# One more weight unit per attention step, and residual loads from another queue, in an attention and ternary-FFN kernel

## The chip, the cores and the metric

The kernel runs on the 8 cores of one Trainium2 chip. Each core computes one of the 8 sequences of the batch; there is no traffic between the cores. The metric is the time on the device of the slowest core, in microseconds.

## The reference

```python
x = L0_attn_x                                  # (8, 2048, 1024), one sequence a core
x = _layernorm(x + attn(x, w_qkv, w_proj, b_proj))     # 16 heads of 64, softmax over 2048 keys
x = _layernorm(x + ffn(x, w_gate, w_up, w_down))
return x

# grouped_linear: 8 groups of 128 channels, used for qkv (128 -> 384) and proj (128 -> 128)
def _weight_quant(w):                          # ternary weights, one scale for a matrix
    scale = 1.0 / clip(mean(abs(w)), 1e-5)
    return clip(round(w * scale), -1, 1) / scale
def _act_quant(x):                             # 8-bit activations, one scale for a token
    scale = 127.0 / clip(max(abs(x), axis=-1), 1e-5)
    return clip(round(x * scale), -128, 127) / scale
def _bitlinear(x, w):
    return einsum('bsi,oi->bso', _act_quant(x), _weight_quant(w))
# ffn: bitlinear(silu(bitlinear(x, w_gate)) * bitlinear(x, w_up), w_down), 1024 -> 4096 -> 1024
```

## The kernel before

The program is written by hand as five queues of instructions. A helper, `Emitter`, records every instruction under its engine, and `replay` (line 84, which is why nearly every row of the profile says L84) issues them. Engines run their own instructions strictly in the order in which they were recorded; what orders them against each other is written out as waits on semaphore counts. A wait marked `future=True` is for a count that is reached by an instruction recorded later. A DMA is issued by one of three engines: "sync" (SyncE, SPq in the profile), "scalar" (ScalarE, ACTq) or "gpsimd" (GpSimd, POOLq). The issue stands in that engine's order too.

A core's 2048 tokens are T = 16 tiles of 128. The stages:

1. Loads, the bias, bf16 copies of `x`, the transposed copy, and the sums of absolute weights (`emit_wmean`) for the scale of each weight matrix. Then q, k and v.
2. Attention, in QC = 4 blocks of 512 queries (`qc`), each in 8 pairs of heads (`p`), each over 16 key tiles (`kc`): TensorE makes scores, ScalarE the exponential of 128x1024 scores, TensorE the product with v. At the end of a `p` ScalarE copies the result out and sends the row sums by a small DMA (`A10`, sums of all heads of the `qc`). After the eight pairs VectorE takes the reciprocal of `A10` and runs the projection's 64 instructions on 128x128 blocks with TensorE, and then the layer norm of four tiles (`emit_ln_quad`), which writes `xp_s` (the residual for the FFN) and `xq_s` (quantised tokens) to HBM through GpSimd's queue. SyncE then loads `xqT`, the transposed `xq_s`. The first scores of the next `qc` come on TensorE after this `qc`'s projection.
3. Weight quantisation, recorded into the attention so that VectorE and SyncE do it between. The weights are 96 units of 128x1024: `_wq_units` in the order wd, wg, wu, 32 of each. `drain_wq(k)` records k of them. A unit is a load by SyncE into one of two halves of `A5` (`emit_wq_load`, recorded two units ahead; it waits until the unit two before is done), three VectorE instructions of 128x1024 (in the profile `TENSOR_SCALAR A<-A,wsc` is the first of the three, so it marks a unit), and a store by SyncE. `drain_wt(k)` records k of 32 transposed loads of quantised wd (`wtstage<-wdq_s`, SyncE), whose blocks GpSimd stores to `wdqT_s`; it returns at once while fewer than 32 units have been recorded. The calls stand at the end of each `p`:

```python
            if qc == wsum_qc and p == 2:     # wsum_qc = 1
                emit_wsum_once()
            if _wsum_done[0] and p < 7:
                drain_wq(6)
            if qc >= 1 and p < 7:
                drain_wt(4)
```

So calls are made at p = 2 to 6 of qc 1 and at p = 0 to 6 of qc 2 and qc 3 while units are left.

4. Gate and up matmuls (`emit_gu`), twice, for 8 tiles of tokens each (s = 0 and 1): `h = silu(gate) * up`, quantised and stored to `hq_s` by ScalarE's queue.
5. Down matmuls and the last layer norm (`emit_down`), in four token groups of four tiles (`gbase` 0 to 3). TensorE runs over 32 weight tiles (`wdt_sb`, loaded by SyncE four ahead, with transposed loads of `hqT` between) into all eight PSUM banks. Then VectorE adds the residual `xre_f` for tile after tile. `xre_f` holds two tiles, so it is loaded in two pairs from `xp_s`: the first pair when the group before has stored its output, the second when VectorE has used the first (`c_r2` counts tiles). Then follow sums, Squares on ScalarE (which overwrite `xre_f`), and the output `y` through `xre_f`. TensorE's next group waits for VectorE's four tiles.

Of the kernel before, what the change touches and what calls it, by code (L numbers as in the profile page):

```python
# [20 lines left out]
class Emitter:  # L21
# [17 lines left out]
    def c(self, name):  # L39
        self.sem(name)  # L40
        return self.cnt[name]
# [11 lines left out]
    def wait(self, eng, semname, val, future=False):  # L53
        if val <= 0:
            return
        self.sem(semname)
        if future:
            self.future_waits.append((eng, semname, val))
        else:
            assert val <= self.cnt[semname], \  # L60
                f"wait {eng} {semname}>={val} but only {self.cnt[semname]} emitted"
        lw = self.last_wait[eng].get(semname, -1)
        if val <= lw:
            return
        self.last_wait[eng][semname] = val
        self.ops[eng].append(("wait_ge", (self.sems[semname], val), {}, None))
# [6 lines left out]
    def dma(self, eng, out, in_, semname, **kw):  # L73
        return self.emit(eng, "dma_start", out, in_, inc=(semname, 16), **kw)
# [20 lines left out]
def build(T=16, NST=2, debug=False, phase=3, attn_lvl=4):  # L95
# [41 lines left out]
    def alloc(name, shape, dtype, at=None):  # L137
        nbytes = int(np.prod(shape[1:])) * mybir.dt.size(dtype)
        nbytes = (nbytes + 31) // 32 * 32
        if at is None:  # L140
            at = off[0]
            off[0] = at + nbytes
        assert at + nbytes <= 229344, f"SBUF overflow: {name}"
        return nc.alloc_sbuf_tensor_at(name, list(shape), dtype, offset=at), at
# [41 lines left out]
    xre_f, _ = alloc("xre_f", [128, 2048], F32, at=A13o)  # L186
# [13 lines left out]
    def bank(i, lo=0, hi=512):  # L200
        return ps[:, 512 * i + lo: 512 * i + hi]
# [4 lines left out]
    E = Emitter(nc, ctx)  # L206
    em, wait, dma, c = E.emit, E.wait, E.dma, E.c
# [175 lines left out]
    def emit_wq_load(gidx):  # L383
        mi, tii, to = _wq_units[gidx]
        par = gidx % 2
        stg = A5[:, par * 1024:(par + 1) * 1024]
        if gidx >= 2:
            wait("sync", "c_wq3", 3 * (gidx - 1), future=True)
        else:
            wait("sync", "c_wma", 96, future=True)  # L390
        dma("sync", stg, tii, f"s_wqp{par}")

    def drain_wq(k):
        for _ in range(k):
            gidx = _wq_emitted[0]
            if gidx >= len(_wq_units):
                return
            _wq_emitted[0] = gidx + 1
            mi, tii, to = _wq_units[gidx]
            par = gidx % 2  # L400
            stg = A5[:, par * 1024:(par + 1) * 1024]
            obuf = A6[:, par * 1024:(par + 1) * 1024]
            if gidx == 0:
                emit_wq_load(0)
                emit_wq_load(1)
            if gidx + 2 < len(_wq_units):
                emit_wq_load(gidx + 2)
            wait("vector", f"s_wqp{par}", 16 * (gidx // 2 + 1))
            wait("vector", "c_wsc", 1)
            wait("vector", "c_wq3", c("c_wq3"))  # L410
            em("vector", "tensor_scalar", stg, stg, wsc[:, mi:mi + 1], 1.0,
               ALU.mult, ALU.min, inc=("c_wq3", 1))
            wait("vector", "c_wq3", c("c_wq3"))
            em("vector", "tensor_scalar", stg, stg, -1.0, MAGIC, ALU.max, ALU.add,
               inc=("c_wq3", 1))
            wait("vector", "c_wq3", c("c_wq3"))
            if gidx >= 2:
                wait("vector", f"s_wqs{par}", 16 * (gidx // 2))
            em("vector", "tensor_scalar", obuf, stg, MAGIC, None, ALU.subtract,
               inc=("c_wq3", 1))  # L420
            wait("sync", "c_wq3", c("c_wq3"), future=True)
            dma("sync", to, obuf, f"s_wqs{par}")
# [224 lines left out]
    for qc in range(QC):  # L647
        for p in range(8):
# [75 lines left out]
            if qc == wsum_qc and p == 2:  # L724
                emit_wsum_once()
            if _wsum_done[0] and p < 7:
                drain_wq(6)
            if qc >= 1 and p < 7:
                drain_wt(4)
            if qc == 0 and p == 2 and attn_lvl in (3, 4):  # L730
# [260 lines left out]
    def emit_down(s):  # L991
        for tg in range(NTG):
            gbase = s * NTG + tg
            row0 = (s * ST + tg * 4) * 128
            wait("gpsimd", "s_xps0", 16 * (T // 2))
            wait("gpsimd", "s_xps1", 16 * (T // 2))
            if gbase >= 1:
                wait("gpsimd", "c_r2", gbase * 4, future=True)
                wait("gpsimd", "c_s", c("c_s"), future=True)
                wait("gpsimd", "s_out0", 16 * 2 * gbase)  # L1000
                wait("gpsimd", "s_out1", 16 * 2 * gbase)
            for t4 in range(2):
                E.dma("gpsimd", xre_f[:, t4 * 1024:(t4 + 1) * 1024],
                      xp_s[row0 + t4 * 128: row0 + (t4 + 1) * 128, :], "s_xre")
            for jc in range(32):
                k = gbase * 2 + jc // 16
# [37 lines left out]
            for t4 in range(4):  # L1044
                tt = s * ST + tg * 4 + t4
                if t4 == 2:
                    wait("gpsimd", "c_r2", gbase * 4 + 2, future=True)
                    for t4b in range(2, 4):
                        E.dma("gpsimd", xre_f[:, (t4b - 2) * 1024:(t4b - 1) * 1024],
                              xp_s[row0 + t4b * 128: row0 + (t4b + 1) * 128, :],  # L1050
                              "s_xre")
                wait("vector", "c_dn", c("c_dn"))
                wait("vector", "c_v", c("c_v"))
                wait("vector", "c_s", c("c_s"))
                wait("vector", "s_xre", 16 * (gbase * 4 + (t4 // 2) * 2 + 2),
                     future=True)
                xrh = xre_f[:, (t4 % 2) * 1024:(t4 % 2 + 1) * 1024]
                em("vector", "scalar_tensor_tensor", B[t4][:, 0:512],
                   bank(t4 * 2), scd[:, tt:tt + 1], xrh[:, 0:512],
                   ALU.mult, ALU.add, inc=("c_dne", 1))  # L1060
                em("vector", "scalar_tensor_tensor", B[t4][:, 512:1024],
                   bank(t4 * 2 + 1), scd[:, tt:tt + 1], xrh[:, 512:1024],
                   ALU.mult, ALU.add, inc=("c_r2", 1))
# [67 lines left out]
    else:  # L1131
        emit_hqt_half(0)
        emit_hqt_half(1)
    emit_down(0)
    if NST > 1:
        emit_down(1)
# [39 lines left out]
```

How the kernel before makes its waits and increments, by code:

```python
                def body(eng):  # L79
                    for meth, args, kw, inc in self.ops[name]:
                        if meth == "wait_ge":
                            eng.wait_ge(*args)
                        else:
                            ins = getattr(eng, meth)(*args, **kw)
                            if inc is not None:
                                ins.then_inc(*inc)
```

## Time and profile before

| | |
|---|---|
| median of 3 runs (lowest, highest) | 2122.22 us (2120.99, 2122.87) |
| the profiled execution | 2119.69 us |
| its span, core 5, the slowest | 2116.7 us |
| spans of the eight cores | 2109.0 to 2116.7 us |
| granted TensorE clock, mean of a core | 0.844 to 0.846 |
| busy share of the span: TensorE, ScalarE, VectorE, GpSimd | 64%, 45%, 44%, 3% |

All rows below are of core 5. A time is in us from the span's start. In the timeline a row is: start, us taken (of all its instructions, if several are merged as x8), engine, line, operation, output<-inputs with shapes, count, and in brackets how long the engine had been idle before it and who ended that. In the table of waits a row is: who waited for whom, us in total, times, the longest. In a row of windows: the stretch, its length, busy us (and instructions) of PE (TensorE), PEld (its weight loads), DVE (VectorE), ACT (ScalarE) and POOL (GpSimd), the granted TensorE clock as a share of full speed, the busy share of the 16 DMA engines, and GB/s. `A` stands for any of the buffers A0 to A15.

### The profile page before, as it was taken

The numbers are of one execution on the slowest core, as the hardware profiler recorded it, in microseconds if no ns is written. First come the engines' busy times: TensorE is split into PE (matmuls) and PEld (weight loads), VectorE is DVE, ScalarE is ACT, GpSimd is POOL, SyncE is SP. The second block draws the span as 40 slices with busy tenths as digits, with TensorE's granted clock in tenths as the row PEclk, the third lists the DMA queues.
The fourth block names the chain that finished last, engine by engine and source line by source line (L and its number), as shares of the span: only waits on it lengthen the run. The fifth ranks groups of instructions, "written<-read, shape, count | busy, mean of one in ns | idle before, by whom it ended". The sixth has DMA issues, their size and how long they took to land.

```text
span 2116.4 us, 20559 instructions; the slowest of 8 cores (2109.0 to 2116.7 us)
## 1 busy us (share of the span) xinstructions
PE 1342.5 (63%) x5439; PEld 463.1 (22%) x5502; DVE 924.7 (44%) x1742; ACT 948.8 (45%) x1079; POOL 53.1 (3%) x100
## 2 busy tenths in 40 slices
PE   0057767576647773067663799945999728676581
PEld 0001111111111110011111344412444313232230
DVE  1138850554567434484518444444444441303123
ACT  2167888488838884058870112264121461001011
POOL 0000000000000000000000000000000000000000
PEclk9999888688868887578875899977999868898896
DMA  6779960135742777836803633334344416676662
GB/s 184 226 232 327 313 208 1 40 100 151 196 138 79 198 226 211 236 98 174 237 23 96 136 76 76 74 107 120 75 95 95 115 82 166 169 205 185 188 201 77
DMA packets 371458, 314.02 MB, mean 148 GB/s; under 512 B 296593, under 2 KB 298641, under 8 KB 369298
## 3 DMA queue, kind: packets, MB, share of 16 engines
q1 hardware_dynamic: 339712, 234.97, 42.4%
q10 hardware_dynamic: 20882, 39.99, 5.5%
q0 software_dynamic: 10752, 37.75, 4.8%
q8 instruction: 47, 0.77, 0.2%
q14 instruction: 65, 0.53, 0.1%
HBM read 161.49 MB, written 83.89 MB: 116 GB/s over the span
## 4 chain that ended last, share of the span: by engine, by line
PE 43%; ACT 15%; DMA 13%; DVE 12%; SPq 7%; issue 7%; ACTq 2%; DVEq 1%; POOL 0%; POOLq 0%
PE ps L84 43%; ACT A L84 14%; DVE A L84 8%; SPq L84 7%; DMA A<-wg 3%; DMA wdt_sb<-wdqT_s 2%; DVE ln_sb L84 2%; DMA wtstage<-wdq_s 2%; ACTq L84 2%; DMA xre_f<-xp_s 1%; DVE h L84 1%; DMA A<-x 1%; DMA wdqT_s<-wtstage 1%; DMA A<-wu 1%; DMA A<-wqkv 1%
## 5 line engine op out<-in xcount | busy, mean ns | idle before, releaser
L84 ACT ACTIVATE A<-ps,cst_sb 128x1024 bf16<-128x1024 f32 (+1 forms) x544 | 553.1, 1103 | 247.2 <-DVE A L84 157.1
L84 PE MATMUL ps<-A,A 64*128 64x512 bf16 (+1 forms) x2048 | 532.3, 434 | 204.3 <-ACT A L84 180.3
L84 PE MATMUL ps<-wg_sl,xqT 128*128 128x512 bf16 x1003 | 264.0, 407 | 114.6 <-DVE h L84 99.6
L84 PE MATMUL ps<-wdt_sb,hqT 128*128 128x512 bf16 x1003 | 238.3, 393 | 107.2 <-DMA wdt_sb<-wdqT_s 47.7
L84 PEld LDWEIGHTS ps<-A,A 64*128 64x128 bf16 (+1 forms) x2048 | 125.7, 106 | 609.0 <-issue 605.7
L84 ACT ACTIVATE A<-ps,scg 128x512 f32<-128x512 f32 x128 | 87.9, 687 | 331.5 <-PE ps L84 309.5
L84 DVE SCALAR_TENSOR_TENSOR h<-ps,scu,A 128x512 bf16<-128x512 f32 x128 | 96.1, 751 | 216.6 <-ACT A L84 212.4
L84 DVE TENSOR_SCALAR A<-A,wsc 128x1024 f32<-128x1024 f32 x96 | 72.3, 753 | 205.4 <-DMA A<-wg 98.0
L84 PEld LDWEIGHTS ps<-wg_sl,xqT 128*128 128x128 bf16 x1024 | 104.0, 103 | 251.7 <-issue 145.6
L84 DVE TENSOR_SCALAR A<-A 128x1024 f32<-128x1024 f32 (+1 forms) x208 | 144.4, 694 | 32.5 <-DVE A L84 18.2
L84 PEld LDWEIGHTS ps<-wdt_sb,hqT 128*128 128x128 bf16 x1024 | 100.2, 100 | 245.3 <-issue 141.4
L84 ACT ACTIVATE xre_f<-A,ln_sb 128x1024 f32<-128x1024 f32 x16 | 18.4, 1147 | 275.3 <-DVE ln_sb L84 275.3
L84 PE MATMUL ps<-wproj_sb,A 64*128 64x128 bf16 x256 | 36.5, 274 | 155.5 <-DVE A L84 155.5
L84 DVE TENSOR_REDUCE wt<-A 128x1 f32<-128x1024 f32 x96 | 117.1, 1220 | 40.0 <-DMA A<-wg 21.0
L84 ACT ACTIVATE A<-h,cst_sb,ln_sb 128x512 f32<-128x512 bf16 x128 | 104.0, 813 | 56.7 <-DVE scd L84 45.9
L84 PE MATMUL ps<-wu_sl,xqT 128*128 128x512 bf16 x501 | 124.3, 389 | 7.6 <-DMA wu_sl<-wuq_s 7.0
L84 DVE SCALAR_TENSOR_TENSOR A<-ps,scd,xre_f 128x512 f32<-128x512 f32 x32 | 21.8, 745 | 244.6 <-PE ps L84 217.4
L84 PE MATMUL ps<-A,wqkv_sb 128*128 128x512 bf16 x63 | 36.7, 586 | 122.4 <-ACT A L84 76.4
L84 ACT CAST A<-ps 64x512 bf16<-64x512 f32 (+2 forms) x144 | 76.1, 536 | 41.0 <-PE ps L84 37.5
L84 DVE TENSOR_REDUCE A<-h 128x1 f32<-128x512 bf16 x128 | 87.8, 686 | 13.6 <-DVE h L84 0.5
L84 DVE SCALAR_TENSOR_TENSOR A<-ps,A,A 128x128 f32<-128x128 f32 x256 | 78.7, 346 | 16.9 <-PE ps L84 3.1
L84 DVE TENSOR_SCALAR h<-A 128x512 bf16<-128x512 f32 x128 | 54.7, 427 | 65.0 <-ACT A L84 64.9
(67 smaller groups left out, 710.2 us busy)
## 6 DMA issues: line engine op xcount, KB each, us to landing
A<-wg SPq DMA_DIRECT2D x64, 512.0 KB, 5.6
A<-wu SPq DMA_DIRECT2D x64, 512.0 KB, 5.4
A<-wd SPq DMA_DIRECT2D x64, 512.0 KB, 6.4
wdt_sb<-wdqT_s SPq DMA_DIRECT2D x128, 256.0 KB, 3.2
hq_s<-h ACTq DMA_DIRECT2D x16, 1024.0 KB, 3.9
A<-x SPq DMA_DIRECT2D x16, 512.0 KB, 6.9
xt_s<-A POOLq DMA_DIRECT2D x16, 512.0 KB, 3.8
A<-xt_s ACTq DMA_DIRECT2D x16, 512.0 KB, 3.3
```

The source lines that it names most:

```text
L84: ins = getattr(eng, meth)(*args, **kw)
```

## The change

Two things change. The number of weight units recorded at the end of each `p` goes from 6 to 7. In `emit_down` the loads of `xre_f`, with the waits ahead of them, move from GpSimd's queue to ScalarE's. There they stand in ScalarE's order: the first pair after the last work of the stage before (for group 0 after the last `hq_s` store, for the others after the `y` stores of the group before), the second pair ahead of the group's Squares. The wait for `c_s`, ScalarE's own count, is kept.

```diff
@@ -724,7 +724,7 @@
             if _wsum_done[0] and p < 7:
-                drain_wq(6)
+                drain_wq(7)
@@ -992,15 +992,15 @@
-            wait("gpsimd", "s_xps0", 16 * (T // 2))
-            wait("gpsimd", "s_xps1", 16 * (T // 2))
+            wait("scalar", "s_xps0", 16 * (T // 2))
+            wait("scalar", "s_xps1", 16 * (T // 2))
             if gbase >= 1:
-                wait("gpsimd", "c_r2", gbase * 4, future=True)
-                wait("gpsimd", "c_s", c("c_s"), future=True)
-                wait("gpsimd", "s_out0", 16 * 2 * gbase)
-                wait("gpsimd", "s_out1", 16 * 2 * gbase)
+                wait("scalar", "c_r2", gbase * 4, future=True)
+                wait("scalar", "c_s", c("c_s"))
+                wait("scalar", "s_out0", 16 * 2 * gbase)
+                wait("scalar", "s_out1", 16 * 2 * gbase)
             for t4 in range(2):
-                E.dma("gpsimd", xre_f[:, t4 * 1024:(t4 + 1) * 1024],
+                E.dma("scalar", xre_f[:, t4 * 1024:(t4 + 1) * 1024],
                       xp_s[row0 + t4 * 128: row0 + (t4 + 1) * 128, :], "s_xre")
@@ -1044,9 +1044,9 @@
                 if t4 == 2:
-                    wait("gpsimd", "c_r2", gbase * 4 + 2, future=True)
+                    wait("scalar", "c_r2", gbase * 4 + 2, future=True)
                     for t4b in range(2, 4):
-                        E.dma("gpsimd", xre_f[:, (t4b - 2) * 1024:(t4b - 1) * 1024],
+                        E.dma("scalar", xre_f[:, (t4b - 2) * 1024:(t4b - 1) * 1024],
                               xp_s[row0 + t4b * 128: row0 + (t4b + 1) * 128, :],
                               "s_xre")
```

## Rows read from the trace of the kernel before

**Rows 1.** The windows of core 5: qc 2, the boundary, qc 3.
```profile
632.00:818.00 186.00, 131.02 (x507) 31.02 (x506) 92.02 (x140) 157.75 (x160) 13.38 (x24) 0.86 0.64 179
818.00:915.00 97.00, 10.37 (x70) 4.42 (x70) 53.31 (x112) 0.05 (x1) 5.93 (x11) 0.50 0.80 213
915.00:1101.00 186.00, 131.55 (x508) 31.07 (x506) 86.46 (x132) 158.02 (x160) 7.23 (x12) 0.84 0.45 133
```

**Rows 2.** ScalarE's timeline, where attention of qc 2 and qc 3 begins.
```profile
631.78 2.12 ACT L84 ACTIVATE A<-ps,cst_sb 128x1024 bf16<-128x1024 f32 x2 [30.22 <-DVE A L84]
...
914.95 2.12 ACT L84 ACTIVATE A<-ps,cst_sb 128x1024 bf16<-128x1024 f32 x2 [97.29 <-DVE A L84]
```

**Rows 3.** Timeline of VectorE (DVE), from qc 2's last unit to its projection.
```profile
887.65 0.75 DVE L84 TENSOR_SCALAR A<-A,wsc 128x1024 f32<-128x1024 f32 x1 [0.78 <-DMA A<-wu]
...
889.99 0.54 DVE L84 RECIPROCAL A<-A 128x64 f32<-128x64 f32 x1
...
891.35 23.09 DVE L84 SCALAR_TENSOR_TENSOR A<-ps,A,A 128x128 f32<-128x128 f32 x64 [0.82 <-PE ps L84]
```

**Rows 4.** Timeline of VectorE: first and last unit of qc 1, then its projection.
```profile
485.98 0.75 DVE L84 TENSOR_SCALAR A<-A,wsc 128x1024 f32<-128x1024 f32 x1 [1.55 <-ACT wsc L84]
...
599.55 0.75 DVE L84 TENSOR_SCALAR A<-A,wsc 128x1024 f32<-128x1024 f32 x1 [2.18 <-DMA A<-wd]
...
606.80 0.55 DVE L84 RECIPROCAL A<-A 128x64 f32<-128x64 f32 x1 [4.83 <-DMA A<-A]
...
608.17 23.10 DVE L84 SCALAR_TENSOR_TENSOR A<-ps,A,A 128x128 f32<-128x128 f32 x64 [0.82 <-PE ps L84]
```

**Rows 5.** Timeline of VectorE: two units of qc 3, and its reciprocal.
```profile
1016.53 0.75 DVE L84 TENSOR_SCALAR A<-A,wsc 128x1024 f32<-128x1024 f32 x1 [0.97 <-DMA A<-wu]
...
1058.12 0.75 DVE L84 TENSOR_SCALAR A<-A,wsc 128x1024 f32<-128x1024 f32 x1 [0.91 <-DMA A<-wu]
...
1103.57 0.55 DVE L84 RECIPROCAL A<-A 128x64 f32<-128x64 f32 x1 [43.02 <-DMA A<-A]
```

**Rows 6.** Timeline of SyncE's queue (SPq) in qc 2 and after it.
```profile
718.83 0.51 SPq L84 DMA_DIRECT2D A<-wg  x1
...
738.65 11.11 SPq L84 DMA_TRANSPOSE wtstage<-wdq_s  x4
...
891.04 13.18 SPq L84 DMA_TRANSPOSE wtstage<-wdq_s  x4
```

**Rows 7.** Timeline of VectorE: second and last unit of one group.
```profile
727.31 0.75 DVE L84 TENSOR_SCALAR A<-A,wsc 128x1024 f32<-128x1024 f32 x1
...
742.15 0.75 DVE L84 TENSOR_SCALAR A<-A,wsc 128x1024 f32<-128x1024 f32 x1 [0.78 <-DMA A<-wg]
```

**Rows 8.** Timeline at the last `xre_f` reload, and the table of waits.
```profile
2078.02 1.07 POOL L84 DMA_DIRECT2D xre_f<-xp_s  x2 [31.15 <-DVE A L84]
...
2083.00 2.73 DVE L84 SCALAR_TENSOR_TENSOR A<-ps,scd,xre_f 128x512 f32<-128x512 f32 x4 [5.52 <-DMA xre_f<-xp_s]
...
DVE A L84 <- DMA xre_f<-xp_s: 29.5, 4, 9.0
```

**Rows 9.** DMA issues (count, KB each, us to landing); `xt_s` issues, min/median/max ns.
```profile
hq_s<-h ACTq DMA_DIRECT2D x16, 1024.0 KB, 3.9
...
A<-xt_s ACTq DMA_DIRECT2D x16, 512.0 KB, 3.2
...
xp_s<-A POOLq DMA_DIRECT2D x16, 512.0 KB, 3.0
...
L84 ACTq DMA_DIRECT2D A<-xt_s x16: 321/326/685, 269.1 to 1116.7; - x16
```

**Rows 10.** Timeline: an instruction of VectorE, the Square that waits for it.
```profile
2090.54 0.17 DVE L84 TENSOR_SCALAR ln_sb<-ln_sb 128x4 f32<-128x4 f32 x1
...
2090.86 1.15 ACT L84 ACTIVATE xre_f<-A,ln_sb 128x1024 f32<-128x1024 f32 x1 [48.66 <-DVE ln_sb L84]
```

**Rows 11.** The window of the first pass of gate and up.
```profile
1175.00:1463.00 288.00, 240.73 (x1024) 103.95 (x1022) 133.28 (x287) 95.04 (x127) 0.00 (x0) 0.91 0.42 91
```

## The prediction

> **What bounds the kernel now.** I read the page first, then the granted clocks, the windows, the chain of waits, and short stretches of the timeline. By the page no engine is full (TensorE, the busiest, has 64% of the span), so a mean says nothing and the stages have to be looked at one by one.
>
> The windows [rows 1] do that. The attention of qc 2 and of qc 3 take 186 us each, with ScalarE busy 158 us of it: the exponentials set the pace there. Between them lie 97 us in which TensorE is busy for 10.37. ScalarE's own idle time shows how odd that boundary is [rows 2]: ScalarE stood 30.22 us before qc 2, but 97.29 us before qc 3, both times for VectorE, though the projection between is the same 64 instructions in 23.1 us [rows 3, 4].
>
> The reason is the weight quantisation. VectorE runs its instructions in order, and the units of `drain_wq` that the program puts into the attention of a qc stand ahead of that qc's reciprocal and projection. In qc 2 there are 7 calls of 6, 42 units. The last starts at 887.65, and the reciprocal follows its third instruction without a gap, at 889.99 [rows 3]. Attention had been over since about 817.7 (914.95 less 97.29). So in qc 2 the quantisation is the path, by 72 us.
>
> In qc 1 the 30 units end just in time [rows 4]: the first starts at 485.98, the last at 599.55, and it is done 2.4 us later, at 602. The reciprocal then waits 4.83 us for the row sums that ScalarE had just sent, and starts at 606.80. The slack there is those 4.83 us and no more. In qc 3 the last unit starts at 1058.12, and the reciprocal comes at 1103.57, after 43.02 us of idling [rows 5].
>
> **Part 1: `drain_wq(7)` for `drain_wq(6)`.** The work is the same 96 units; only where they stand changes. Before: 5 x 6 = 30 in qc 1, 7 x 6 = 42 in qc 2, 24 in qc 3. After: 35, 49 and 12. That is 5 more in the qc that has 4.83 us of slack, 7 more in the qc that has none, and 12 fewer in the one that had 43 us to spare.
>
> *qc 1.* The rate is 29 intervals in 113.57 us, 3.92 us a unit [rows 4]. Units of wu, in qc 3, run quicker: 12 intervals from 1016.53 to 1058.12, 3.47 us [rows 5]. Of the five, units 30 and 31 are of wd and 32 to 34 of wg, so I take 3.8. Five units are 19.0 us, less the slack of 4.83: **+14.2 us**. The bounds are 5 x 3.47 - 4.83 = 12.5 and 5 x 3.92 - 4.83 = 14.8.
>
> *qc 2.* Here SyncE's queue alternates between the loads and stores of six units and four transposes of `drain_wt(4)` [rows 6]: one group begins at 718.83, its transposes come at 738.65 and hold the queue 11.11 us, and the next group begins at 749.85, 31 us after the first. While the transposes hold the queue no unit is loaded, and VectorE has a hole of over 10 us. One could think the seventh unit free in that hole. It is not: with two staging halves a load is issued only when the unit two before it is done, and the transposes stand in the queue behind the last load and store of the group. A seventh unit pushes the transposes back by one interval, and the hole comes after it, as long as before. The interval inside this group is (742.15 - 727.31) / 4 = 3.71 us [rows 7]; without transposes it is 3.47 [rows 5]. I take 3.6, between the two. Seven groups have one unit more each: **+25.2 us**, with the bounds 7 x 3.47 = 24.3 and 7 x 3.92 = 27.4.
>
> *The transposes.* `drain_wt` does nothing until 32 units are emitted. That is now so at p = 6 of qc 1, so 4 of the 32 transposes move there; 28 stay in qc 2, as before, and the 4 of qc 3 are gone. The moved four stand behind unit 34's store in SyncE's queue and run beside the projection of qc 1. Behind them in that queue is the load of `xqT`, which waits for the end of the layer norm anyway, over 25 us of VectorE's work later. The projection is not slowed by such company: four transposes, from 891.04 on, ran beside that of qc 2, whose 64 instructions took 23.09 us, and those of qc 1 took 23.10 without them [rows 3, 4, 6]. GpSimd stores three of the moved blocks before its next work, the `xp_s` stores of that layer norm. I cost all this at nothing, and keep 3 us as an upper bound.
>
> *qc 3.* The 186 us of attention cover 12 units as they covered 24: nothing.
>
> **Part 2: the loads of `xre_f` go from GpSimd's queue to ScalarE's.** There are 16 loads in 8 pairs. The first pair of each token group is far from the path: it is needed only after the group's 32 weight tiles. In groups 1 to 3 it waits for the output stores on either engine, and ScalarE's next work, the Square, comes after those matmuls too. In group 0 it moves from before the gate and up matmuls to behind ScalarE's last `hq_s` store, where its 1 MB shares the DMA engines with the first tiles of `wdt_sb`. I cost it at nothing, and at up to 3 us if TensorE waits for most of such a transfer (3.9 us [rows 9]).
>
> The second pair is on the path four times: VectorE stands 29.5 us for it in all, 9.0 the longest and 5.52 the last [rows 8], and TensorE's next group stands behind VectorE. What can be saved of a stand: GpSimd begins its issue 0.53 us after VectorE ends (2077.49 to 2078.02 [rows 8]; the stand is 5.52 before 2083.00), where ScalarE begins 0.15 us after VectorE (2090.71 to 2090.86 [rows 10]): 0.4 us. An issue takes 0.54 us on GpSimd (1.07 for two) and 0.33 on ScalarE, two of each: 0.4 us [rows 8, 9]. Together 0.8 us, four times: **-3.2 us**. Behind ScalarE's new wait for `c_r2` stands only the Square, which needs later sums of VectorE: the wait costs nothing. The ends: if the pair took only the 3.9 us that the 1 MB `hq_s` store takes from ScalarE's queue [rows 9], plus 0.5 us to start, the four stands would be 17.6 us instead of 29.5, -12. If ScalarE's issues suffered as the slowest `xt_s` issue did, 0.69 us instead of 0.33, that would be two of 0.36 us in each pair, 4 x 0.7, and if nothing else were gained, +3.
>
> Here the Trainium skill ("DMA: Bandwidth & Descriptors", Specifications) gives a first-byte latency of about 1 us for GpSimd's path and about 0.6 us for that of SyncE and ScalarE. By that, an estimate from the page, each pair would win another 0.4 us and part 2 would be -4.8. The trace shows no such difference: 512 KB land in a median of 3.0 us from GpSimd's issue (`xp_s`) and in 3.2 us from ScalarE's (`xt_s`) [rows 9].
>
> **Sum.** +14.2 + 25.2 - 3.2 = +36.2 us. The profiled execution took 2119.7 us (span 2116.7 and 3 us around it), so it would be 2155.9. The median of the runs, 2122.2, stands 2.5 us above it: 2158.4, and I say **2158 us**, 1.7% slower.
>
> **Rivals.**
>
> *A. The seventh unit fills the hole.* If the extra load could be in flight while the transposes run, part 1 would cost nothing in qc 2, and 14.2 - 3.2 = +11 remained: 2133. For it: the hole in each group. Against it: the order of the queue, above. 5%.
>
> *B. The throttle gives the time back.* TensorE idles 39 us longer before the gate and up matmuls, whose granted clock is 0.91 [rows 11]. If rest bought clock later, their two passes of 240 us could give back some 5%, 24 us: 2134. Against it: after 97 us of near idleness the attention of qc 3 was granted 0.84, no more than the 0.86 of qc 2, which followed 29 us [rows 1]. 4%.
>
> *C. Contention makes it dearer.* The DMA engines are busy 80% in the last groups of qc 2 [rows 1]. Units of 4.5 us, 0.6 over the mean of qc 1, would make 5 x 4.5 - 4.8 + 7 x 4.5 = +49; with 3 us each for the moved transposes and group 0, and part 2 taken off, +52: 2174. 9%.
>
> *D. Faster.* The reload pairs save the 12 us of their far end while part 1 costs nothing. That decides only if something other than the last unit ends the boundaries, as a wait on the row sums would, so that 5 and 7 units are free: 2110. Rows 3 speak against it: no gap stands between the last unit and the reciprocal. 3%.
>
> *E. No change*: a gain from part 2 and a part 1 that is mostly hidden cancel, 2122. The same rows speak against it. 3%.
>
> The forecast has 76%; its own range is 2150 to 2166, part 1 from 34.9 to 42.2 and part 2 from -8 to +1. The range for 8 in 10 reaches a little toward C and toward the far end of part 2: **2146 to 2168**. A measurement of this kernel tells about 0.2%, 4 us, from no change. Slower by more than that: 0.94 (the forecast, A, B, C); the same 0.03; faster 0.03.
>
> **What would show it.** In the profile of the changed kernel ScalarE's idle time grows from 30.2 to about 44 us before qc 2 and from 97.3 to about 122 us before qc 3; the reciprocal of qc 1 follows the last unit without a wait; each group on SyncE's queue has seven loads and lasts about 35 us; VectorE idles over 80 us before the reciprocal of qc 3; and the stands for `xre_f` shrink by about 0.8 us each. I am wrong if a group still lasts 31 us (A), if the granted clock of the gate and up stage rises (B), if the groups last 36 us and more (C), or if the stands for `xre_f` fall to 4 or 5 us, which makes part 2 three times what I took.

## The result and the profile after

The changed kernel took 2162.35 us, the median of 8 runs (2157.21 to 2168.23); the kernel before, on the same chips, 2125.04 us (8 runs, 2120.88 to 2130.19). The ratio is 1.0173 with a 95% interval of 1.0153 to 1.0194: slower by 1.7%. The prediction said 2158 us, 1.7% slower, range 2146 to 2168; it stood on the first median of the kernel before, 2122.2 us, which is 2.8 us lower than this one. The profiled execution took 2159.01 us. Its slowest core is core 6, span 2156.1 us, where before it was core 5 with 2116.7; the mean of the eight spans went from 2113.4 to 2149.1 us.

The windows of the changed kernel, core 6: the attention of qc 2, the boundary, the attention of qc 3, and the first pass of gate and up. The columns are those of [rows 1].

```profile
646.00:833.00 187.00, 131.75 (x508) 31.10 (x506) 97.45 (x148) 157.82 (x160) 12.23 (x21) 0.86 0.63 180
833.00:958.00 125.00, 9.94 (x68) 4.29 (x68) 62.58 (x125) 0.00 (x0) 8.43 (x15) 0.50 0.74 209
958.00:1144.00 186.00, 132.12 (x508) 31.24 (x508) 61.26 (x97) 157.16 (x160) 4.74 (x8) 0.84 0.23 71
1220.00:1508.00 288.00, 232.14 (x998) 101.87 (x1016) 131.50 (x284) 95.31 (x127) 0.00 (x0) 0.91 0.40 91
```

Attention takes 186 to 187 us as before, and its clock on this core is the same 0.86 and 0.84. The boundary has grown from 97 us [rows 1] to 125, and TensorE is busy there for 9.94 us, no more than before. Gate and up are granted 0.91, as in [rows 11].

ScalarE's timeline at the two boundaries, as in [rows 2].

```profile
646.06 2.12 ACT L84 ACTIVATE A<-ps,cst_sb 128x1024 bf16<-128x1024 f32 x2 [45.02 <-DVE A L84]
...
958.62 2.12 ACT L84 ACTIVATE A<-ps,cst_sb 128x1024 bf16<-128x1024 f32 x2 [125.70 <-DVE A L84]
```

45.02 us where there were 30.22, and 125.70 where there were 97.29. VectorE's timeline says why (columns as in [rows 3]): the last unit of qc 1 and the reciprocal behind it, the same for qc 2, then the reciprocal of qc 3.

```profile
618.68 0.75 DVE L84 TENSOR_SCALAR A<-A,wsc 128x1024 f32<-128x1024 f32 x1 [0.97 <-DMA A<-wg]
...
621.02 0.55 DVE L84 RECIPROCAL A<-A 128x64 f32<-128x64 f32 x1
...
931.15 0.75 DVE L84 TENSOR_SCALAR A<-A,wsc 128x1024 f32<-128x1024 f32 x1 [0.64 <-DMA A<-wu]
...
933.49 0.54 DVE L84 RECIPROCAL A<-A 128x64 f32<-128x64 f32 x1
...
1147.49 0.55 DVE L84 RECIPROCAL A<-A 128x64 f32<-128x64 f32 x1 [94.91 <-DMA A<-A]
```

In qc 1 the wait of 4.83 us ahead of the reciprocal [rows 4] is gone: now VectorE comes last there too. In qc 3 the reciprocal waits 94.91 us where it waited 43.02 [rows 5]; 12 units fewer and four transposes fewer have emptied a qc that had room already.

SyncE's queue, one group of qc 2 from its first load to the first load of the next, and VectorE's second and last unit of that group, which answer to [rows 6, 7].

```profile
724.85 11.07 SPq L84 DMA_TRANSPOSE wtstage<-wdq_s  x4
...
736.01 0.53 SPq L84 DMA_DIRECT2D A<-wg  x1
...
758.88 11.58 SPq L84 DMA_TRANSPOSE wtstage<-wdq_s  x4
...
770.55 0.53 SPq L84 DMA_DIRECT2D A<-wg  x1
```

```profile
741.14 0.75 DVE L84 TENSOR_SCALAR A<-A,wsc 128x1024 f32<-128x1024 f32 x1 [10.39 <-DMA A<-wg]
...
743.73 0.75 DVE L84 TENSOR_SCALAR A<-A,wsc 128x1024 f32<-128x1024 f32 x1 [0.16 <-DVE A L84]
...
762.85 0.75 DVE L84 TENSOR_SCALAR A<-A,wsc 128x1024 f32<-128x1024 f32 x1 [1.49 <-DMA A<-wg]
```

The group is 770.55 - 736.01 = 34.5 us long, where it was 31. Its transposes take 11.58 us in the queue, where they took 11.11, and VectorE's hole ahead of 741.14 is still there. Five intervals from 743.73 to 762.85 are 3.82 us each.

Three places of the timeline: the late first pair of `xre_f` loads, the end of VectorE's first wait for the matmuls of group 0, and the last reload.

```profile
1796.86 1.66 ACTq L84 DMA_DIRECT2D xre_f<-xp_s  x2
...
1860.71 2.73 DVE L84 SCALAR_TENSOR_TENSOR A<-ps,scd,xre_f 128x512 f32<-128x512 f32 x4 [64.30 <-PE ps L84]
...
2115.16 2.73 DVE L84 SCALAR_TENSOR_TENSOR A<-ps,scd,xre_f 128x512 f32<-128x512 f32 x4 [44.40 <-PE ps L84]
...
2117.96 0.81 ACTq L84 DMA_DIRECT2D xre_f<-xp_s  x2
...
2122.58 2.73 DVE L84 SCALAR_TENSOR_TENSOR A<-ps,scd,xre_f 128x512 f32<-128x512 f32 x4 [4.70 <-DMA xre_f<-xp_s]
```

From the view of the tile `xre_f`, the issues of its 16 loads (min/median/max ns, first and last start):

```profile
L84 ACTq DMA_DIRECT2D xre_f<-xp_s x16: 326/455/1177, 1796.9 to 2118.3; - x16
```

And the table of waits, as in [rows 8]:

```profile
DVE A L84 <- DMA xre_f<-xp_s: 26.4, 4, 8.0
```

The last issue begins 0.07 us after VectorE ends (2115.16 + 2.73 = 2117.89) and takes 0.81 us for two; it was 0.53 and 1.07 [rows 8]. The last stand is 4.70 us instead of 5.52, and the four are 26.4 instead of 29.5. But the matmuls of group 0 kept VectorE waiting 64.30 us. In the kernel before they did so for 61.29 us, as this row of its VectorE shows:

```profile
1815.00 2.73 DVE L84 SCALAR_TENSOR_TENSOR A<-ps,scd,xre_f 128x512 f32<-128x512 f32 x4 [61.29 <-PE ps L84]
```

One core is one sample, so this table has the means over the eight cores of each profiled execution (lowest and highest in brackets), of the four rows above in every core. The experiments below are read from it too.

| kernel | ScalarE idle before qc 2 | before qc 3 | stands for `xre_f`, sum | wait for group 0 | span |
|---|---|---|---|---|---|
| before | 29.8 (27.7-32.1) | 96.3 (94.1-97.8) | 29.0 | 61.9 (61.0-63.0) | 2113.4 |
| changed | 40.4 (37.5-45.0) | 120.3 (116.4-125.7) | 26.2 | 64.5 (64.1-65.7) | 2149.1 |
| p1_only | 40.5 (39.2-43.5) | 120.6 (119.3-122.7) | 29.6 | 61.8 (61.3-62.3) | 2148.5 |
| q1_only | 41.1 (36.7-45.3) | 96.4 (92.7-98.1) | 29.8 | 62.2 (61.5-63.3) | 2127.5 |
| q2_only | 29.5 (27.7-30.8) | 121.9 (119.3-127.7) | 29.5 | 62.1 (61.9-62.8) | 2142.3 |
| p2_only | 28.2 (27.7-30.1) | 98.4 (97.1-100.1) | 26.3 | 64.8 (63.3-66.3) | 2116.4 |
| p2_only_b | 29.2 (27.7-31.0) | 97.0 (91.8-99.4) | 26.1 | 66.1 (64.2-69.7) | 2113.4 |
| p2_group0_early | 30.1 (28.8-31.9) | 99.3 (97.1-103.7) | 26.9 | 61.8 (61.4-62.1) | 2114.5 |
| p2_group0_early_b | 28.2 (27.7-29.7) | 98.7 (96.8-101.6) | 26.7 | 62.0 (61.5-62.7) | 2112.9 |
| wt_between | 29.6 (27.7-31.4) | 72.7 (66.8-78.0) | 29.2 | 62.1 (61.5-62.6) | 2091.3 |
| five_in_q2 | 29.5 (27.7-31.3) | 74.4 (72.8-76.6) | 29.3 | 62.0 (61.5-62.8) | 2092.6 |
| combined | 29.5 (27.7-30.7) | 52.0 (45.5-60.7) | 26.7 | 62.2 (61.2-63.7) | 2070.1 |
| balanced | 28.6 (27.7-30.7) | 35.3 (32.4-38.0) | 26.4 | 62.9 (61.7-64.5) | 2053.4 |

From before to changed: +10.6 + 24.0 - 2.8 + 2.6 = +34.4 us, and the mean span grew by 35.7. These four places hold all but 1.3 us of the difference.

### The profile page after: what moved, and what is told of

Same layout as the page of the kernel before. It is cut to its first block, busy times and chain, and to the rows that moved or that the text cites. A ratio compares the mean times of both kernels' runs of the same rounds, so it can differ in the third digit from the quotient of the medians.

```text
span 2156.1 us, 20545 instructions; the slowest of 8 cores (2141.8 to 2156.1 us)
## 1 busy us (share of the span) xinstructions
PE 1338.7 (62%) x5439; PEld 463.2 (21%) x5502; DVE 924.6 (43%) x1742; ACT 947.9 (44%) x1079; POOL 45.0 (2%) x84
## 4 chain that ended last, share of the span: by engine, by line
PE 39%; DMA 18%; DVE 14%; ACT 13%; SPq 7%; issue 7%; ACTq 2%; DVEq 1%; POOLq 0%
PE ps L84 39%; ACT A L84 12%; DVE A L84 10%; SPq L84 7%; DMA A<-wg 3%; DMA A<-wd 2%; DMA A<-wu 2%; DMA wdt_sb<-wdqT_s 2%; DVE ln_sb L84 2%; DMA wtstage<-wdq_s 2%; ACTq L84 2%; DMA A<-wqkv 1%; DMA wdq_s<-A 1%; DMA xre_f<-xp_s 1%; DVE h L84 1%
## 5 line engine op out<-in xcount | busy, mean ns | idle before, releaser
L84 DVE TENSOR_SCALAR A<-A,wsc 128x1024 f32<-128x1024 f32 x96 | 72.3, 753 | 197.7 <-DMA A<-wu 76.6
L84 PE MATMUL ps<-A,wqkv_sb 128*128 128x512 bf16 x63 | 36.7, 586 | 122.8 <-ACT A L84 74.8
L84 ACT CAST A<-ps 64x512 bf16<-64x512 f32 (+2 forms) x144 | 76.2, 536 | 40.9 <-PE ps L84 37.5
```

The lines of the kernel that those rows point to most:

```text
L84: ins = getattr(eng, meth)(*args, **kw)
```

## The experiments

### Each part alone

p1_only is the kernel before with the first hunk of the diff alone:

```diff
-                drain_wq(6)
+                drain_wq(7)
```

> Part 1 alone: drain_wq(7), the xre_f loads on GpSimd's queue as before. My theory (five units past the slack of qc 1, seven units in qc 2, which has none): 36 to 40 us slower than before, ratio 1.017 to 1.019, ScalarE's idle time before qc 2 some 41 to 45 us and before qc 3 some 120 to 125 us. Rival (the two parts act on each other, as by DMA traffic): its distance from before differs by more than 4 us from that of the full change plus 3 us.

Measured: 2165.71 us against 2127.33, ratio 1.0186 (1.0170 to 1.0201). The boundaries are those of the changed kernel within 0.3 us in the mean. Part 1 is the whole slowdown: the full change measured 1.0173 (1.0153 to 1.0194), and the two intervals overlap. The rival that the parts act on each other falls.

p2_only is the changed kernel with `drain_wq(6)`, run a second time as p2_only_b.

> Part 2 alone: drain_wq(6) as before, the xre_f loads on ScalarE's queue. My theory (each of the four stands for xre_f is 0.8 us shorter): 3 us faster than before, ratio 0.9985, the stands 26 to 27 us in all instead of 29.5. Rival (first-byte latency of about 1 against 0.6 us, the Trainium skill, DMA: Bandwidth & Descriptors, adds its 0.4 us a pair): 5 us faster. Rival (the moved first pair disturbs the first weight tiles of the down stage): 0 to 3 us slower in that group, no change in all.

Measured: ratio 0.9993 (0.9978 to 1.0008). The stands shrank by 2.7 us, but no gain could be told. (p2_only_b, below, gave 1.0001.) In the trace TensorE's first group had become longer: 64.8 us instead of 61.9, on all eight cores outside the range of before. That was the place I had priced at nothing, with 3 us as its bound.

### The two places of part 1

```diff
-                drain_wq(6)
+                drain_wq(7 if qc == 1 else 6)      # q1_only
+                drain_wq(7 if qc == 2 else 6)      # q2_only
```

> 7 units a call in qc 1 alone (35, then 42 and 19), loads of xre_f as before. The four transposes move into the boundary of qc 1, as in the changed kernel. My theory: only the slack of qc 1 is overrun, 10 to 15 us slower, ratio 1.005 to 1.007; ScalarE's idle time before qc 2 is 40 to 45 us and before qc 3 stays at 96 to 97. Rival (the moved transposes cost too): 3 us more, seen in a projection of qc 1 longer than 23.1 us.

Measured: ratio 1.0055 (1.0037 to 1.0074), 11.7 us. Of core 7, the slowest, ScalarE's timeline:

```profile
648.97 2.12 ACT L84 ACTIVATE A<-ps,cst_sb 128x1024 bf16<-128x1024 f32 x2 [43.63 <-DVE A L84]
...
934.01 2.12 ACT L84 ACTIVATE A<-ps,cst_sb 128x1024 bf16<-128x1024 f32 x2 [98.13 <-DVE A L84]
```

Only the first boundary grew (+11.3 us in the mean), though qc 2 had the same 42 units as ever and the four transposes ran in that boundary. The projection beside them took 23.1 us as ever; VectorE's timeline of this core has it in two pieces, 645.52 + 2.94 - 625.30 = 23.16:

```profile
623.93 0.55 DVE L84 RECIPROCAL A<-A 128x64 f32<-128x64 f32 x1
...
625.30 20.04 DVE L84 SCALAR_TENSOR_TENSOR A<-ps,A,A 128x128 f32<-128x128 f32 x56 [0.82 <-PE ps L84]
...
645.52 2.94 DVE L84 SCALAR_TENSOR_TENSOR A<-ps,A,A 128x128 f32<-128x128 f32 x8 [0.18 <-issue]
```

From the reciprocal to ScalarE's next exponential it is 25.2 us in the mean of the eight cores, where it was 25.0. So the moved transposes cost some 0.2 us.

> 7 units a call in qc 2 alone (30, then 49 and 17), loads of xre_f as before. My theory (a seventh unit pushes the transposes back by one interval, 3.4 to 4.1 us in each of 7 groups): 24 to 28 us slower, ratio 1.011 to 1.013, the boundary before qc 2 unchanged at 28 to 32 us and that before qc 3 120 to 125 us. Rival A of the prediction (the seventh unit fills the hole left by the transposes): no change.

Measured: ratio 1.0118 (1.0100 to 1.0135), 25.1 us; the boundary before qc 3 is 121.9 us in the mean, +25.6, the one before qc 2 unchanged. Rival A, the hole that takes the seventh unit for nothing, falls. The two alone add to 1.73%; part 1 measured 1.86%, the change 1.73%.

### Where part 2's gain went

p2_group0_early is part 2 with one pair of loads left where it was:

```diff
+            e0 = "gpsimd" if gbase == 0 else "scalar"
-            wait("scalar", "s_xps0", 16 * (T // 2))
-            wait("scalar", "s_xps1", 16 * (T // 2))
+            wait(e0, "s_xps0", 16 * (T // 2))
+            wait(e0, "s_xps1", 16 * (T // 2))
...
-                E.dma("scalar", xre_f[:, t4 * 1024:(t4 + 1) * 1024],
-                      xp_s[row0 + t4 * 128: row0 + (t4 + 1) * 128, :], "s_xre")
+                E.dma(e0, xre_f[:, t4 * 1024:(t4 + 1) * 1024],
+                      xp_s[row0 + t4 * 128: row0 + (t4 + 1) * 128, :],
+                      "s_xre" if gbase else "s_xre0")
```

VectorE's waits, not shown here, count the two semaphores accordingly.

> Part 2 without its first pair of group 0: that pair goes back to GpSimd's queue and its early place (on a semaphore of its own, s_xre0), the other seven pairs stay on ScalarE's queue, drain_wq(6). In part 2 alone the matmuls of group 0 kept VectorE waiting 64 to 66 us instead of 61 to 63. My theory (the late pair shares the DMA engines with the first weight tiles and costs 2.7 us, the four stands save 3): that wait is back at 61 to 63 us, the stands stay at 25 to 28 us, and it is 2.5 to 3.5 us faster than before, ratio 0.9985 to 0.999. Rival (the longer wait in group 0 comes from elsewhere, as from clock or from ScalarE's later queue): the wait stays at 64 us or more and the ratio is 0.9993 to 1.

Measured: the wait for group 0 was back at 61.8 us and the stands stayed at 26.9, as expected, but the ratio, 1.0000, had an interval of 0.9964 to 1.0035 and decided nothing. So both kernels ran once more on one chip.

> The same kernel as p2_group0_early once more, because the interval of that run (0.9964 to 1.0035) was too wide; now on one chip with part 2 alone. My theory: 2.5 to 3.5 us faster than before (0.9985 to 0.999) and 2 to 3 us faster than part 2 alone, with the wait of VectorE for group 0 at 61 to 63 us. Rival: both the same as before within 1 us.

> Part 2 alone once more, beside p2_group0_early_b on one chip. My theory (3 us saved in the four stands, 2.7 us lost in group 0): the same as before within 1 us, ratio 0.9993 to 1. Rival (only the stands count, as the prediction had it): 3 us faster, 0.9985.

Measured: p2_group0_early_b 0.9983 (0.9971 to 0.9995), p2_only_b 1.0001 (0.9991 to 1.0011). First the slowest core of p2_only_b: VectorE's first wait in the timeline, then TensorE's line in the table of waits.

```profile
1820.53 2.73 DVE L84 SCALAR_TENSOR_TENSOR A<-ps,scd,xre_f 128x512 f32<-128x512 f32 x4 [69.69 <-PE ps L84]
```

```profile
PE ps L84 <- DMA wdt_sb<-wdqT_s: 53.7, 33, 6.6
```

The same two views of the slowest core of p2_group0_early_b:

```profile
1820.34 2.72 DVE L84 SCALAR_TENSOR_TENSOR A<-ps,scd,xre_f 128x512 f32<-128x512 f32 x4 [61.85 <-PE ps L84]
```

```profile
PE ps L84 <- DMA wdt_sb<-wdqT_s: 45.6, 30, 8.2
```

The two tables of waits are of one core each and of all four groups. In group 0 alone, over the eight cores, TensorE waited for `wdt_sb` 13.4 us in the mean in p2_only and 14.0 (11.8 to 16.3) in p2_only_b; with that pair back in its early place it was 10.9 and 10.0 (9.3 to 11.4), and in the kernel before 10.8 (9.6 to 12.4). So the late first pair, behind the last `hq_s` store, makes TensorE wait some 3 to 4 us more for `wdt_sb`, and VectorE 4.1 us more for TensorE (66.1 against 62.0, p2_only_b and p2_group0_early_b).

The ratios alone show this weakly: p2_group0_early_b is 3.6 us (0.17% of 2123.87) faster than the kernel before, with an interval of 1 to 6 us, where part 2 was forecast to give 3.2, and its interval touches that of p2_only_b. The traces say it more sharply. From the start of the reciprocal of qc 3 to the end of the span, past all that part 1 touches, the mean of the eight cores is 1011.7 to 1013.7 us in the six kernels with the loads as before, 1011.1 to 1014.1 in the three with the whole of part 2, and 1009.6 to 1011.1 in the four with the first pair early (combined and balanced, below, are two of them): 2.5 us less than as before in the mean. What the late pair takes from the weight tiles, the DMA engines' time or a place in the order, was not separated.

### What sets the pace in qc 2

Two runs test the account of the group from the other side, by making it shorter. five_in_q2 takes a unit out of each call in qc 2:

```diff
-                drain_wq(6)
+                drain_wq((0, 6, 5, 6)[qc])
```

> 5 units a call in qc 2 instead of 6 (30, 35 and 31 units), all else as before. My theory (each unit of qc 2 costs about 3.5 us on the path, and qc 3 has 43 us to spare): 23 to 26 us faster than before, ratio 0.988 to 0.989; the boundary before qc 3 is 71 to 74 us, and the wait ahead of the reciprocal of qc 3 falls from 43 to about 20 us. Rival (the pace of qc 2 is set by the seven groups of transposes, not by the units): less than 10 us faster.

Measured: ratio 0.9874 (0.9850 to 0.9897), 26.8 us faster. The boundary fell by 21.9 us in the mean, 3.1 us a unit (the mean span by 20.8; the ratio is that of the slowest cores, over more executions). The reciprocal of qc 3 waited 13.7 to 19.5 us where it had waited 43: seven more units fitted there and cost nothing. The rival, groups paced by their transposes alone, falls.

wt_between changes the order alone:

```diff
-                drain_wq(6)
-            if qc >= 1 and p < 7:
-                drain_wt(4)
+                for u in range(6):
+                    drain_wq(1)
+                    if u < 4:
+                        drain_wt(1)
```

> The kernel before with one transposed load put behind each of the first four units of a call instead of four behind the last; 6 units a call, part 2 undone. My theory (in qc 2 the order of SyncE's queue sets the pace: four transposes in a row wait for one another's stores and keep loads from being issued): the boundary before qc 3 falls from 97 us by 30 to 45 us, as the groups shrink from 31 to 25 or 26 us, where the DMA engines, busy 0.8 of a group now, would be full; ratio 0.979 to 0.986. Rival (the groups are bound by what the DMA engines and HBM carry, whatever the order): no change. Rival (each transpose between delays its neighbours by as much as four in a row do): no change either, but with the DMA share below 0.85.

Measured: ratio 0.9875 (0.9852 to 0.9898), 26.6 us faster; the boundary fell by 23.6 us, less than the 30 to 45 that I expected. So the order does matter, but not as far. The windows over most of qc 2's pass, of before (core 5) and of wt_between (core 3), show the limit in the last two columns, the busy share of the DMA engines and GB/s:

```profile
700.00:890.00 190.00, 81.64 (x314) 19.31 (x314) 81.31 (x115) 99.63 (x101) 12.95 (x24) 0.72 0.81 221
```

```profile
700.00:870.00 170.00, 82.11 (x314) 19.34 (x314) 81.75 (x115) 98.85 (x100) 14.76 (x25) 0.74 0.95 258
```

0.81 and 221 GB/s before, 0.95 and 258 GB/s now; over the eight cores the share is 0.79 to 0.81 before and 0.88 to 0.98 now. So the order was what held the pass back, up to 24 us. That the DMA engines then end the gain is what this share suggests. It is not shown: SyncE's queue still stood 27 to 37 us in this window for GpSimd's stores of transposed blocks.

### A version that beats both

combined is wt_between with five units a call in qc 2 and with part 2 as in p2_group0_early:

```diff
-                for u in range(6):
+                for u in range((0, 6, 5, 6)[qc]):
```

> 5 units a call in qc 2, one transpose behind each of the first four units, the loads of xre_f on ScalarE's queue except the first pair of group 0. My theory: the gains add as long as the boundary before qc 3 stays above the 28 us that the projection and its waits need; groups of 22 to 23 us make it 28 to 45 us, so 55 to 72 us faster than before with the 3 us of part 2, ratio 0.966 to 0.974. Rival (the DMA engines are full before that): 40 us or less, ratio above 0.981.

Measured: ratio 0.9776 (0.9755 to 0.9796), 47.7 us faster, between my range and the rival's (the mean span fell by 43.3 us). The boundary is 52.0 us, not 28 to 45: from 690 to 850 us of core 0 the DMA engines are busy 0.94, so they may pace the units that are left. The reciprocal of qc 3 still waits 23.6 to 29.7 us. balanced moves seven more units into that room, with `(0, 6, 4, 6)`.

> The combined kernel with 4 units a call in qc 2 instead of 5 (30, 28 and 38 units). My theory (a unit costs what it takes in the qc without slack, and nothing in a qc with slack): the boundary before qc 3 falls from 46 to 61 us by up to 28 us, to 28 to 33 us on most cores, while qc 3 takes 7 units more, 24 us, against 24 to 30 us of slack, so its reciprocal waits some 0 to 6 us; 18 to 24 us faster than the combined kernel, 64 to 70 us faster than before, ratio 0.967 to 0.970. Rival (qc 3 becomes the new bound, as its later units interleave with more DMA traffic): the boundary after qc 3 grows past its 27 us by 5 us or more and the ratio is above 0.971.

Measured: ratio 0.9735 (0.9714 to 0.9755), 56 us faster than the kernel before and 4.3% under the changed one (0.9735 / 1.0173). That is short of the 64 to 70 us that I expected, and the ratio is above the 0.971 that I gave the rival. The rival's cause, a new bound in qc 3 worth 5 us or more, is there only in small: from the first exponential of qc 3 to its reciprocal it is 190.1 us in the mean where it was 188.6, and from that reciprocal to the end of VectorE's wait for group 0 712.9 where it was 711.4. In qc 2 the boundary is 35.3 us, over the 28 to 33 that I expected: the last seven units taken out gave 16.7 us, 2.4 each, where the first seven gave 3.1. The load of the DMA engines doesn't explain that. From 690 to 818 us they are busy 0.82 to 0.91 over the eight cores, less than in combined, while SyncE's queue stands 61 to 65 of these 128 us for GpSimd's stores of transposed blocks. The 28 transposes that balanced leaves in qc 2 may by now set the pace; no run moved them.

On core 2, the slowest, the reciprocal of qc 3 waits 1.09 us:

```profile
1043.30 0.75 DVE L84 TENSOR_SCALAR A<-A,wsc 128x1024 f32<-128x1024 f32 x1 [1.32 <-DMA A<-wu]
...
1046.81 0.55 DVE L84 RECIPROCAL A<-A 128x64 f32<-128x64 f32 x1 [1.09 <-DMA A<-A]
```

Over the eight cores it waits 3.44 us at most, and on two of them not at all. The room in qc 3 is used up. A further unit moved there should cost about its interval, 3.5 us (an estimate from [rows 5]), and save less than that in qc 2; that wasn't tried.

## Why the prediction was right

**The bound.** That the quantisation, not attention, ends qc 2 was right: the reciprocal follows the last unit without a gap in both kernels, and ScalarE's idle time at the two boundaries grew by 34.6 us of the 35.7 in the mean span.

**The term of qc 1, +14.2 us.** Right in kind, too large by 3.6 us in the mean (10.6; q1_only 11.3). I took the slack of core 5, 4.83 us; the waits ahead of that reciprocal in the eight cores of before are 1.61 to 7.62 us, 5.35 in the mean. And I took 3.8 us for each added unit: the five take 3.63 us each in the mean of the eight cores, 18.1 us. The rest, 2.0 us, lies in the thirty units ahead of them, whose 29 intervals take 110.6 us in the mean and not 112.6. Nothing in the change explains that; the same thirty units take 109.7 us in p2_only and 112.0 in p2_only_b, so it is the spread from one execution to another. 18.1 - 2.0 - 5.35 = 10.8. On core 6, which came to be the slowest, it was +14.8 over core 5, and +12.9 over core 6 itself (32.14 before).

**The term of qc 2, +25.2 us.** 24.0 in the mean of the changed kernel, 25.6 in q2_only, 28.4 from core 5 before to core 6 after. The seventh unit costs its interval, and the hole stays as long as it was.

**The moved transposes, nothing.** Right within 0.2 us: in q1_only the stretch beside them, from the reciprocal to the next exponential, is 25.2 us instead of 25.0.

**Part 2's stands, -3.2 us.** -2.8 in the mean. The last pair (core 5 before, core 6 after) gave 0.82 us: 0.46 us of it is the earlier start, 0.26 the shorter issues, where I had 0.4 and 0.4, and 0.1 is left over. The Trainium skill ("DMA: Bandwidth & Descriptors", Specifications) would have had another 0.4 us a pair from the first byte: the stands of the eight cores give 0.7 us a pair in all, so the trace doesn't show it here.

**Part 2's first pair, nothing with 3 us as a bound.** This step was wrong, and the bound was the value: +2.6 us in the mean, with every core above all eight of before. I argued that the pair itself is needed only after the 32 weight tiles, which is true, and gave no price to what it delays. But TensorE waits for `wdt_sb` again and again in this stage (45.6 us in all in the table of waits of p2_group0_early_b, and in group 0 of the kernel before 9.8 us in seven waits on core 5), so what delays a tile is on the path. It turned a gain of 3 us into none. The two errors, -3.6 in qc 1 and +2.6 here, nearly cancel in the mean: that the sum came so close is partly luck.

**Sum.** +36.2 us forecast; +35.7 in the mean span, +39.4 in that of the slowest core of the profiled executions, 36.8 by the ratio. The lower end of part 1 in the forecast's own range, 34.9, is not the sum of its bounds, which is 12.5 + 24.3 = 36.8; nor do -8 and +1 for part 2 follow from its ends, -12 and +3. The outcome lies inside either way.

**The rivals.** A fell by q2_only. B, the throttle, fell: the first pass of gate and up was granted 0.89 to 0.91 over the eight cores, 0.90 to 0.91 before, and the stretch from the reciprocal of qc 3 to the end of VectorE's wait for group 0, which holds both passes, is 711.2 us in the mean in p1_only and 711.4 before. C was there a little on the slowest core, with intervals of 3.82 us. D and E fell with p1_only.

## What to carry to other kernels

When background work is dealt out over stages, what counts is each stage's slack, read as the wait ahead of the instruction that joins it with the main work: in these runs one more unit cost its full interval where that wait was nil and nothing where it was long, so an even share is the wrong share. A hole in an engine's timeline is not room; ask which queue would have to issue into it. And a load that is moved to a later place "off the path" must be priced by what it is moved in front of: here it took back all that the faster queue had won.

## What was not expected of the hardware

On core 6 of the changed kernel two issues of 512 KB loads in a row took 0.81 to 0.84 us on ScalarE's queue, with SyncE's transposes beside them or without (the last pair has none); but the pair right behind the 1 MB `hq_s` store took 1.66 us, one of the two 1.18. Over the eight cores that pair took 0.95 to 1.80 us; why is open. GpSimd's two took 1.07 [rows 8]. And in this mix of 512 KB loads, 256 KB stores and transposes the order of one queue was worth 37 GB/s: the 16 DMA engines moved 221 GB/s at a busy share of 0.81, and 258 GB/s at 0.95 once the transposes stood between the units.
